# A graph-network kernel on one core: a 25-group ring of source indices, resident destinations, one-hots a group ahead, and the edge products computed during the sums and reloaded in the attention

## The chip, the cores and the metric

The kernel runs on one core of one Trainium2 chip. The metric is device time in microseconds (us); lower is better. The kernel before was timed in three runs: median 12,565.92 us, from 12,555.83 to 12,591.74.

## The reference, cut to what matters

12,500 nodes with 64 features; 400,000 edges, sorted by destination, with 64 attributes each.

```python
def sage_conv(x, src, dst, W_l, b_l, W_r, n_nodes):      # called twice, with a relu between
    msgs = x[src]
    agg = segment_sum(msgs, dst, n_nodes)
    cnt = segment_sum(ones, dst, n_nodes)
    return (agg / maximum(cnt, 1.0)[:, None]) @ W_l.T + b_l + x @ W_r.T

def attention(x, edge_attr, src, dst):                   # 4 heads of 16
    Q, K, V, Ee = x @ Wq.T + bq, x @ Wk.T + bk, x @ Wv.T + bv, edge_attr @ We.T + be
    score = exp(clip((K[src] * Q[dst] * 0.25 * Ee).sum(-1), -5, 5))
    return segment_sum(V[src] * score[..., None], dst, n)

x = layernorm(x + two_sage_convs(x)); out = layernorm(x + attention(x, edge_attr))
```

## The kernel before, in words

A group is 640 edges: 5 for each of the 128 partitions (K = 5). There are 625 groups, in 125 turns of SLOTS = 5, so every buffer that a group uses has five copies, its slots. Nodes are kept on chip in 98 blocks of 128. Since edges are sorted by destination, most groups touch one block of destinations; some touch more. A table made at the start tells each engine a group's first block and how many more it has (97 extra pairs of group and block in all).

The program has three passes over all groups, with dense layers between them.

- **First sum** (`sum_x`) and **second sum** (`sum_h`). SP loads the group's source and destination indices (`edge_ids`). GpSimd (POOL) issues five indirect DMAs, one for each of the five edges of a partition; each gathers 128 rows of a table in DRAM (`x_rows`, then `h_rows`) by the source indices. VectorE (DVE) makes a one-hot matrix `hot` of the destinations inside the block: a subtraction into `dst_local` (L694), then a comparison with `iota` (L695). TensorE (PE) multiplies one-hot and rows, five matmuls (L373). DVE reduces the result (L714), counts degrees in the first sum alone (L716), adds it to the nodes (L717), and goes on to the next pair of group and block. All in one loop (L706) over blocks.
- **Attention** (`att`). POOL gathers K and V rows (`kv_rows`). SP loads indices and edge attributes (`attr`). PE transposes the attributes (L413) and the one-hots (L417), multiplies the attributes by `we2` (L432, L436), fetches the destinations' Q rows by a product with the one-hots (L441, L424), and sums the messages (L446). ScalarE (ACT) copies the transposed pieces and takes the exponent. DVE computes K*Q (L811), times the edge product from PSUM (`kqe`, L812), a reduction (L814), the clip (L815), the one-hot of the group after next (L694, L695), the add to the nodes (L827), and the messages (L820).

Semaphores set the order. `group_done`, counted up by DVE at a group's end, lets SP load the indices of the group that takes the slot; their landing (`ids[u]`) lets POOL gather, and the landing of the five gathers (`got[u]`) lets PE (in the sums) or DVE (in the attention) use them.

## Time and profile before

| what | value |
|---|---|
| median of three timed runs | 12,565.92 us |
| span of the profiled execution | 16,241.9 us |
| its stretches: first sum, second sum, attention | 4,912, 4,898 and 5,978 us |
| what lies before, between and behind them | 459 us |
| POOL busy | 9,186 us (57%) |
| PE busy | 5,274 us (32%) |
| DVE busy | 5,077 us (31%) |

No timed duration of the profiled execution is given beside its span of 16,241.9 us. The span is 29% above the median of the timed runs, so a share of this span is not a share of the timed one. Durations of single instructions, and the distances between them where nothing waits, can be read from it.

### The profile page before, as it was taken

Reading aid. Unit: us, or ns where it says so; the run is one execution under the profiler, and the core shown is the slowest. Engines: PE = TensorE matmul, PEld = TensorE weight load, DVE = VectorE, ACT = ScalarE, POOL = GpSimd, SP = SyncE. Lnnn points to the kernel's source line nnn. Section 1 sums busy time; section 2 is a strip of 40 time slices with the busy share of each in tenths; the row PEclk is TensorE's granted clock in tenths of the full one; section 3 lists DMA queues with packets and bytes.
Section 4 is the critical chain, followed back from the end, with each engine's and each line's share of the span. In section 5 each row is a group of like instructions: output and inputs, shape, how many; then the busy total and the mean of one; then the engine's idle time right before and its main releaser. Section 6 shows DMA issues by size and latency. Waiting matters only on the chain.

```text
span 16241.9 us, 175208 instructions
## 1 busy us (share of the span) xinstructions
PE 5273.6 (32%) x37310; PEld 4336.0 (27%) x37311; DVE 5077.4 (31%) x12457; ACT 1546.3 (10%) x3498; POOL 9186.2 (57%) x9383
## 2 busy tenths in 40 slices
PE   0111111111112111111111113655565566666665
PEld 0000000000002000000000002555555555555555
DVE  3222222222223222222222223333333333333444
ACT  0000000000001000000000000222222222222222
POOL 4666666665564666666656564455555555555554
PEclk9999999999999999999999999766666666666666
DMA  2111111111111111111111111222222122121211
GB/s 50 32 33 32 33 33 32 33 32 31 31 32 36 33 33 32 32 32 32 32 30 32 31 32 27 57 54 54 53 53 54 51 52 52 50 52 49 53 50 50
DMA packets 716290, 649.53 MB, mean 40 GB/s; under 512 B 470247, under 2 KB 566151, under 8 KB 716152
## 3 DMA queue, kind: packets, MB, share of 16 engines
q0 software_dynamic: 300000, 512.60, 13.9%
q1 hardware_dynamic: 416277, 136.79, 3.8%
q8 instruction: 5, 0.08, 0.0%
q14 instruction: 8, 0.07, 0.0%
HBM read 629.36 MB, written 19.26 MB: 40 GB/s over the span
## 4 chain that ended last, share of the span: by engine, by line
issue 31%; DVEq 22%; PE 16%; another core or an unknown queue 15%; DVE 14%; ACT 2%; ACTq 0%; DMA 0%; POOL 0%; SPq 0%; POOLq 0%
DVEq L706 7%; DVE hot L695 5%; PE ps_sum L373 4%; PE ps_sum L446 3%; DVEq L694 3%; DVE part_sum L714 2%; DVE dst_local L694 2%; DVEq L610 2%; DVEq L244 2%; PE ps_e L436 1%; DVEq L712 1%; DVEq L717 1%; PE ps_t L413 1%; DVEq L713 1%
## 5 line engine op out<-in xcount | busy, mean ns | idle before, releaser
L335 POOL DMA_INDIRECT kv<-kv_rows,edge_ids x3125 | 3142.6, 1006 | 3025.2 <-DMA edge_ids<-in_edges 2149.1
L373 PE MATMUL ps_sum<-rows,hot 128*128 128x193 bf16 x7220 | 1396.9, 359 | 8500.1 <-DVE hot L695 5728.5
L335 POOL DMA_INDIRECT rows<-h_rows,edge_ids x3125 | 3025.5, 968 | 1995.7 <-DMA edge_ids<-in_edges 1052.9
L335 POOL DMA_INDIRECT rows<-x_rows,edge_ids x3125 | 3017.1, 965 | 1963.0 <-DMA edge_ids<-in_edges 1001.7
L373 PEld LDWEIGHTS ps_sum<-rows,hot 128*128 128x128 bf16 x7220 | 850.7, 132 | 9045.9 <-issue 9001.2
L694 DVE TENSOR_SCALAR dst_local<-edge_ids,base 128x5 bf16<-128x5 int32 x2265 | 570.4, 252 | 4372.6 <-issue 4337.7
L695 DVE TENSOR_TENSOR hot<-dst_local,iota 128x640 bf16<-128x640 bf16 x2071 | 1713.9, 828 | 377.7 <-issue 249.7
L446 PE MATMUL ps_sum<-message,node_h 128*128 128x64 f32 x6260 | 1203.6, 352 | 272.2 <-issue 235.5
L446 PEld LDWEIGHTS ps_sum<-message,node_h 128*128 128x128 f32 x6260 | 1131.1, 267 | 313.8 <-issue 255.0
L714 DVE TENSOR_REDUCE part_sum<-ps_sum 128x64 f32<-128x192 f32 x1444 | 516.6, 358 | 1924.1 <-issue 1135.8
L550 ACT COPY attrT<-ps_t 128x384 f32<-128x384 f32 x626 | 300.6, 480 | 3295.6 <-remote 1776.6
L436 PE MATMUL ps_e<-we,attrT 128*128 128x128 f32 x2256 | 484.0, 374 | 318.5 <-ACT attrT L550 174.7
L811 DVE TENSOR_TENSOR kq<-kv,ps_q 128x320 f32<-128x320 f32 x375 | 182.9, 488 | 1268.5 <-remote 711.0
L413 PE MATMUL ps_t<-ident,attr 128*128 128x128 f32 x1878 | 480.8, 375 | 273.2 <-issue 266.0
L436 PEld LDWEIGHTS ps_e<-we,attrT 128*128 128x128 f32 x2256 | 457.5, 280 | 354.2 <-ACT attrT L550 193.0
L827 DVE TENSOR_TENSOR node_x<-node_x,ps_sum 128x64 f32 x626 | 137.9, 220 | 1161.1 <-remote 1024.4
L516 ACT ACT_TABLE_LOAD x14 | 18.0, 1283 | 5000.5 <-DVE node_x L725 5000.3
L555 ACT COPY hotT<-ps_hot 128x640 bf16<-128x640 bf16 x626 | 435.4, 696 | 509.5 <-remote 479.8
L516 ACT COPY stage<-node_h 128x896 f32 x14 | 13.2, 943 | 4939.7 <-DVE node_h L725 4939.7
L559 ACT CAST node_h<-hot 128x640 f32<-128x640 bf16 x626 | 447.8, 715 | 0.0
L417 PE MATMUL ps_hot<-ident,hot 128*128 128x128 bf16 x3130 | 407.6, 274 | 90.2 <-issue 83.1
L436 PE MATMUL ps_kv<-we,attrT 128*128 128x128 f32 x1500 | 322.7, 375 | 176.7 <-issue 97.3
(153 smaller groups left out, 6594.4 us busy)
## 6 DMA issues: line engine op xcount, KB each, us to landing
attr<-in_edge_attr SPq DMA_DIRECT2D x627, 160.0 KB
rows<-x_rows,edge_ids POOLq DMA_INDIRECT x3125
rows<-h_rows,edge_ids POOLq DMA_INDIRECT x3125
kv<-kv_rows,edge_ids POOLq DMA_INDIRECT x3125
edge_ids<-in_edges SPq DMA_DIRECT2D x1877, 5.0 KB
kv_rows<-node_h SPq DMA_DIRECT2D x14, 448.0 KB, 3.0
x_rows<-node_q SPq DMA_DIRECT2D x14, 336.0 KB, 2.6
h_rows<-node_q SPq DMA_DIRECT2D x14, 336.0 KB, 2.6
```

What stands on the lines that cost most here:

```text
L335: nc.gpsimd.indirect_dma_start(out=into[:, u, k, 0:width], out_offset=None, in_=table_rows, in_offset=bass.IndirectOffsetOnAxis(ap=edge_id ...
L373: mm = nc.tensor.matmul(ps_sum[:, 0:ROW + 1], hot[:, 0, k, :], rows[:, u, k, 0:ROW + 1], start=(k == 0), stop=(k == K - 1))
L413: tp = nc.tensor.transpose(ps_t[:, i * P:(i + 1) * P], attr[:, u, i * P:(i + 1) * P], ident[:])
L417: tp = nc.tensor.transpose(ps_hot[:, k * P:(k + 1) * P], hot[:, u, k, :], ident16[:])
L436: mm = nc.tensor.matmul(ps_edge[u % 2][:, i * P:(i + 1) * P], attrT[:, i, :], we2[:], start=False, stop=(i == PAIRS - 1))
L446: mm = nc.tensor.matmul(to, one_hots[:, k, :], messages[:, k, :], start=(k == 0), stop=(k == K - 1))
L555: nc.scalar.copy(hotT[:], ps_hot[:, 0:K * P].rearrange("p (i j) -> p i j", i=K)).then_inc(p.hot_c, 1)
L559: nc.scalar.copy(hot32[:, u], hot[:, u])
L694: s.link(v.tensor_scalar(dst_local[:], edge_ids[:, u, K:2 * K], base[:, bass.ds(b, 1)], None, ALU.subtract))
L695: v.tensor_tensor(into, dst_local[:].rearrange("p (k o) -> p k o", o=1).to_broadcast([P, K, P]), iota[:].rearrange("p (o n) -> p o n", o=1 ...
L706: with dve.Fori(0, more + 1) as j:
L714: s.link(v.tensor_reduce(part_sum[:], ps_sum[:, 0:ROW].rearrange("p (s f) -> p f s", s=SPLIT), AX, ALU.add))
```

## The change

**Indices.** The source indices come into a ring of 25 groups (`src_ids`), loaded five groups at a time. The destinations of all groups stay on chip (`dst_ids`, loaded once during the first sum, 25 groups at a time after the first 50). POOL now waits for the slot (`group_done`) itself.

**One-hots.** `one_hot` is one instruction, a scalar_tensor_tensor (subtract, is_equal), in place of two. In the sums it fills the slot of the next group, where before there was one buffer; extra blocks have a path of their own (`hotT`, `ps_extra`).

**Edge products.** Transposes, products and their copies move from the attention into the sums: three groups of edges a turn in the first sum, two a turn in the second. ACT copies the product out of PSUM and stores it to `ee_rows` in DRAM (160 KB a group). The attention loads it back into `ee_in`, in place of the attributes. `kq` takes the space of `attrT`, and `rows` that of `kv`.

```diff
-        edge_ids = sb("edge_ids", [P, SLOTS, 2 * K], I32)
+        src_ids = sb("src_ids", [P, RING, K], I32)
+        dst_ids = sb("dst_ids", [P, (G + AHEAD) * K], I32)
...
             def gather(p, phase, table_rows, into, width):
+                with pool.Fori(0, BIG) as T:
+                    for j in range(SUBS):
+                        pool.wait_ge(ids_in, T * (16 * SUBS) + 16 * (phase * TURNS + j + 1))
+                        for u in range(SLOTS):
+                            at = j * SLOTS + u
+                            pool.wait_ge(p.group_done, T * RING + at + 1)
...
-                        pool.wait_ge(p.ids[u], t * 16 + 16)
...
+                        g = t * SLOTS + u
                         pe.wait_ge(p.got[u], t * (16 * K) + 16 * K)
+                        pe.wait_ge(p.added, g + 1)
+                        pe.wait_ge(p.hot, g + 1)
                         hold(pe)
-                        with pe.Fori(0, more + 1) as j:
...
+                        sum_group(ps_main[u], hot[:, u], u, p.summed)
...
+                        e = first_e + t * per + u
+                        if 0 < u <= per:
+                            edge_products(e - 1)
+                        if u < per:
+                            turn_attr(u, e, (phase * TURNS) * 16 + t * 16 + 16)
...
+            def edge_tiles(first_e, per, turns_before):
+                with act.Fori(0, TURNS) as t:
+                    for i in range(per):
+                        e = first_e + t * per + i
+                        act.wait_ge(ee_turned, e + 1)
+                        act.wait_ge(ee_made, e + 1)
+                        nc.scalar.copy(attrT[:], ps_t[:, 0:PAIRS * P].rearrange("p (i j) -> p i j", i=PAIRS)).then_inc(ee_copied, 1)
+                        act.wait_ge(ee_made, e + 2)
+                        nc.scalar.copy(ee_out[:, i, :], ps_e[:, 0:K * D]).then_inc(ee_ready, 1)
+                        act.wait_ge(ee_ready, e + 2)
+                        nc.scalar.dma_start(ee_v[:, bass.ds(e, 1), :].rearrange("p a c -> p (a c)"), ee_out[:, i, :]).then_inc(ee_stored[i], 16)
...
-            def one_hot(u, b, s, into, ready):
-                s.link(v.tensor_scalar(dst_local[:], edge_ids[:, u, K:2 * K], base[:, bass.ds(b, 1)], None, ALU.subtract))
-                v.tensor_tensor(into, dst_local[:].rearrange("p (k o) -> p k o", o=1).to_broadcast([P, K, P]),
-                                iota[:].rearrange("p (o n) -> p o n", o=1).to_broadcast([P, K, P]), ALU.is_equal).then_inc(ready, 1)
+            def one_hot(g, b, into, ready):
+                v.scalar_tensor_tensor(into, dst_ids[:, bass.ds(g * K, K)].rearrange("p (k o) -> p k o", o=1).to_broadcast([P, K, P]),
+                                       base[:, bass.ds(b, 1)], iota[:].rearrange("p (o n) -> p o n", o=1).to_broadcast([P, K, P]),
+                                       ALU.subtract, ALU.is_equal).then_inc(ready, 1)
...
+            def sum_turn(p, t, nodes, count_edges):
+                words = group_words(ENG.DVE, t, 0, SLOTS + 1)
+                for u in range(SLOTS):
+                    before, first, more = words[u]
+                    g = t * SLOTS + u
+                    one_hot(g + 1, block_at(words[u + 1][1]), hot[:, (u + 1) % SLOTS], p.hot)
+                    dve.wait_ge(p.added, g + 2)
+                    dve.wait_ge(p.summed, g + 1)
+                    add_rows(block_at(first), ps_main[u], nodes, count_edges, p.step, g + 1, p.added)
...
-                v.tensor_tensor(kqe[:], kq[:], ps_edge[u % 2][:, 0:K * D].rearrange("p (k f) -> p k f", k=K), ALU.mult).then_inc(p.scored, 1)
+                v.tensor_tensor(kqe[:], kq, ee_in[:, u], ALU.mult).then_inc(p.scored, 1)
```

How instructions stand on the engines at the places that matter. DVE in the first sum, from one group's add to the next one-hot; ISA and REGISTER_ALU are the sequencer's own steps. Before:

```order
L717 TENSOR_TENSOR node_x<-node_x,part_sum 128x64
L706 REGISTER_ALU x3
L706 COMPARE_AND_BRANCH
L719 ISA
L706 UNCONDITIONAL_BRANCH [waits sx_ids1]
L706 ISA
L694 REGISTER_ALU
L694 ISA
L694 TENSOR_SCALAR dst_local<-edge_ids,base 128x5
L610 ISA
L695 TENSOR_TENSOR hot<-dst_local,iota 128x640 [waits sx_step]
```

After, at the same place (the extra blocks' path between L836 and L847 is jumped over when there are none):

```order
L839 COMPARE_AND_BRANCH
L836 UNCONDITIONAL_BRANCH
L847 ISA
L812 ISA
L812 REGISTER_ALU
L812 ISA
L812 SCALAR_TENSOR_TENSOR hot<-dst_ids,base,iota 128x640
L833 REGISTER_ALU
L818 TENSOR_REDUCE part_sum<-ps_q 128x64 [waits sx_summed,sx_added]
```

The loop head, the wait for indices and the small subtraction have gone from between the add and the one-hot.

PE in the first sum, from the landing of the gathered rows on. Before:

```order
L367 UNCONDITIONAL_BRANCH [waits sx_got1]
L367 ISA
L373 MATMUL ps_sum<-rows,hot 128x193 [waits sx_hot,sx_added]
L373 MATMUL ps_sum<-rows,hot 128x193 x4
L367 REGISTER_ALU x3
```

After (`edge_space` holds the attributes):

```order
L475 REGISTER_ALU [waits sx_got1]
L444 MATMUL ps_q<-kv,hot 128x193 [waits sx_added,sx_hot]
L444 MATMUL ps_q<-kv,hot 128x193 x4
...
L459 MATMUL ps_e<-be_parts,ones 128x384 [waits ee_ready]
L460 REGISTER_ALU
L462 MATMUL ps_e<-we,attrT 128x128 [waits ee_copied]
L462 MATMUL ps_e<-we,attrT 128x128 x2
L453 MATMUL ps_t<-ident,edge_space 128x128 [waits ee_copied,attr_in1]
L453 MATMUL ps_t<-ident,edge_space 128x128 x2
```

One loop head less stands ahead of the group's matmuls, and the edge work stands behind them.

DVE in the attention, after the change:

```order
L1010 REGISTER_ALU [waits att_ee0]
L953 TENSOR_TENSOR attrT<-kv,ps_q 128x320 [waits att_query]
L726 ISA
L954 TENSOR_TENSOR kqe<-attrT,edge_space 128x320 [waits att_step]
L955 REGISTER_ALU
L956 TENSOR_REDUCE score<-kqe 128x20 [waits att_scored]
L726 REGISTER_ALU
L957 TENSOR_SCALAR clipped<-score 128x20 [waits att_step]
```

The same order as before up to the clip, but `kqe` now reads both its inputs from on-chip memory (`attrT` holds `kq`, `edge_space` holds `ee_in`), where the second was PSUM; behind the clip stands the single one-hot instruction.

## Rows read from the trace of the kernel before

**Rows 1.** Groups of instructions by line, POOL's three.

```profile
L335 POOL DMA_INDIRECT kv<-kv_rows,edge_ids x3125 | 3142.6, 1006 | 3025.2 <-DMA edge_ids<-in_edges 2149.1 <-issue 876.1
L335 POOL DMA_INDIRECT rows<-h_rows,edge_ids x3125 | 3025.5, 968 | 1995.7 <-DMA edge_ids<-in_edges 1052.9 <-issue 942.8
L335 POOL DMA_INDIRECT rows<-x_rows,edge_ids x3125 | 3017.1, 965 | 1963.0 <-DMA edge_ids<-in_edges 1001.7 <-issue 961.3
```

**Rows 2.** The chain of waits, one of DVE's sequencer steps in the first sum.

```profile
3006.08 0.70 DVEq L713
```

**Rows 3.** Timeline, POOL alone, first and last of twelve gathers in a row.

```profile
105.39 0.95 POOL L335 DMA_INDIRECT rows<-x_rows,edge_ids  x1 [0.30 <-issue]
...
119.16 0.95 POOL L335 DMA_INDIRECT rows<-x_rows,edge_ids  x1 [0.30 <-issue]
```

**Rows 4.** Windows before, between and behind the three passes.

```profile
0.00:88.00 88.00, 0.87 (x6) 0.67 (x7) 52.65 (x84) 0.02 (x1) 1.07 (x8) 1.00 0.44 112
4981.00:5091.00 110.00, 71.51 (x319) 63.77 (x319) 69.15 (x124) 43.81 (x42) 0.94 (x1) 1.00 0.16 45
10003.00:10217.00 214.00, 159.49 (x608) 140.87 (x608) 113.87 (x231) 60.71 (x114) 0.15 (x1) 1.00 0.11 31
16195.00:16242.00 47.00, 0.00 (x0) 0.00 (x0) 29.70 (x50) 7.92 (x13) 0.00 (x0) 0.50 0.31 68
```

**Rows 5.** Timeline of the second sum, one group's round on three engines.

```profile
5106.25 1.11 POOL L335 DMA_INDIRECT rows<-h_rows,edge_ids  x1 [0.31 <-issue]
...
5109.45 0.97 PE L373 MATMUL ps_sum<-rows,hot 128*128 128x193 bf16 x5 [5.45 <-DMA rows<-h_rows,edge_ids]
...
5110.52 0.36 DVE L714 TENSOR_REDUCE part_sum<-ps_sum 128x64 f32<-128x192 f32 x1 [3.98 <-issue]
5111.03 0.23 DVE L717 TENSOR_TENSOR node_h<-node_h,part_sum 128x64 f32 x1
...
5112.13 0.83 DVE L695 TENSOR_TENSOR hot<-dst_local,iota 128x640 bf16<-128x640 bf16 x1
...
5112.67 1.11 POOL L335 DMA_INDIRECT rows<-h_rows,edge_ids  x1 [0.30 <-issue]
```

**Rows 6.** Timeline of the first sum, one group's round on PE and DVE.

```profile
102.78 0.97 PE L373 MATMUL ps_sum<-rows,hot 128*128 128x193 bf16 x5 [68.62 <-issue]
...
105.57 0.82 DVE L695 TENSOR_TENSOR hot<-dst_local,iota 128x640 bf16<-128x640 bf16 x1
```

**Rows 7.** Timeline of the attention: first group's last gather and use, a blocked gather.

```profile
10223.41 0.95 POOL L335 DMA_INDIRECT kv<-kv_rows,edge_ids  x1 [0.31 <-issue]
...
10226.21 0.49 DVE L811 TENSOR_TENSOR kq<-kv,ps_q 128x320 f32<-128x320 f32 x1 [5.17 <-DMA kv<-kv_rows,edge_ids]
...
10504.72 0.48 DVE L820 TENSOR_TENSOR message<-kv,weight 128x320 f32<-128x320 f32 x1
10504.92 1.11 POOL L335 DMA_INDIRECT kv<-kv_rows,edge_ids  x1 [0.30 <-issue]
```

**Rows 8.** Timeline of the attention, one group's round on DVE without waits.

```profile
10256.94 0.48 DVE L811 TENSOR_TENSOR kq<-kv,ps_q 128x320 f32<-128x320 f32 x1
10257.46 0.49 DVE L812 TENSOR_TENSOR kqe<-kq,ps_e 128x320 f32<-128x320 f32 x1
...
10258.50 0.18 DVE L815 TENSOR_SCALAR clipped<-score 128x20 f32<-128x20 f32 x1
10258.86 0.23 DVE L694 TENSOR_SCALAR dst_local<-edge_ids,base 128x5 bf16<-128x5 int32 x1 [0.18 <-issue]
10259.12 0.82 DVE L695 TENSOR_TENSOR hot<-dst_local,iota 128x640 bf16<-128x640 bf16 x1
...
10260.03 0.49 DVE L820 TENSOR_TENSOR message<-kv,weight 128x320 f32<-128x320 f32 x1
```

**Rows 9.** Timeline, end of the program: a scalar_tensor_tensor.

```profile
16210.31 0.63 DVE L735 SCALAR_TENSOR_TENSOR node_x<-total,node_x 128x448 f32 x1
```

**Rows 10.** Windows, the attention as a whole.

```profile
10217.00:16195.00 5978.00, 3653.52 (x29202) 3285.20 (x29202) 2315.07 (x5500) 1433.87 (x3328) 3142.61 (x3125) 0.65 0.20 52
```

More of the change, by code:

```diff
@@ L193, in __init__ @@
                 self.step = sem(f"{name}_step")
-                if name == "att":
-                    self.attr_t = sem("att_attr_t")
-                    self.attr_c = sem("att_attr_c")
-                    self.edge = sem("att_edge")
+                if name != "att":
+                    self.x_hot, self.x_summed, self.x_added, self.x_step = (
+                        sem(f"{name}_x_{n}") for n in ("hot", "summed", "added", "step"))
+                else:
+                    self.ee = [sem(f"att_ee{u}") for u in range(SLOTS)]
                     self.hot_t = sem("att_hot_t")
@@ L285, in load_edges, with feed_attention, products @@
+            def feed_attention(p):
+                for i, count in enumerate((2 * TURNS, 2 * TURNS, TURNS)):
+                    sp.wait_ge(ee_stored[i], 16 * count)
+                loads = SUBS + 2 * TURNS
+                def products(t):
                     for u in range(SLOTS):
                         sp.wait_ge(p.group_done, t * SLOTS + u + 1)
-                        sp.dma_start(edge_ids[:, u, :], edges_v[:, bass.ds(t * SLOTS + u, 1), :].rearrange("p a c -> p (a c)")).then_inc(p.ids[u], 16)
@@ L298, in _ @@
-            store_rows(d_split, x_rows_v, node_q)
-            load_edges(sum_x)
+                        sp.dma_start(ee_in[:, u].rearrange("p k f -> p (k f)"),
+                                     ee_v[:, bass.ds(t * SLOTS + u, 1), :].rearrange("p a c -> p (a c)")).then_inc(p.ee[u], 16)
+                products(0)
+                with sp.Fori(0, BIG - 1) as T:
+                    for j in range(SUBS):
+                        t = T * SUBS + j + 1
+                        products(t)
+                        load_sources(j, t - 1 + SUBS, t - 1 + loads)
@@ L300, in _ @@
+                with sp.Fori(TURNS - SUBS + 1, TURNS) as t:
+                    products(t)
             sp.wait_ge(be_stored, 16)
@@ L633, in _ @@
             v.engine_nop().then_inc(att.scored, 1)
+            for s in (ee_copied, ee_made, ee_ready, sum_x.added, sum_h.added, sum_x.x_added, sum_h.x_added):
+                v.engine_nop().then_inc(s, 1)
             v.engine_nop().then_inc(extra.added, 1)
```

298 lines of the change are left out of this document (177 added, 121 removed).

## The prediction

> **What bounds the kernel now.** I read the groups of instructions first, then the windows between the passes, then the timeline.
>
> POOL is the busiest engine, with 9,375 indirect DMAs, five a group in each pass. The reader is to see both columns of [rows 1]: means of 965, 968 and 1,006 ns, and idle time before them that is mostly put down to the landing of `edge_ids`, 1,001.7 + 1,052.9 + 2,149.1 = 4,204 us. Read by itself this says: take the wait for the indices away. But the span is 16,242 us and the timed median 12,566 us, so at least 3,676 us of this execution are not in the timed runs. The chain of waits shows where such time sits: in some stretches each step of DVE's sequencer takes 0.70 us, as [rows 2], and the groups behind them end late. `group_done` and the index loads are late with them, so POOL's waits for indices are this execution's symptom.
>
> So I build the timed run from POOL running freely. Twelve gathers in a row start from 105.39 to 119.16 us, 1.252 us apart (about 0.947 busy, 0.305 between) [rows 3]. 9,375 x 1.252 = 11,737 us. Outside the passes POOL stands still for 88 + 110 + 214 + 47 = 459 us [rows 4]. Sum 12,196 us. The median is 12,566, so 370 us are left for all waits and slow gathers together: 370 / 1,875 = 0.20 us a group and pass. POOL is at work in 93% of the timed run. The profiled execution checks this: its gathers took 9,185.2 us against 9,375 x 0.947 = 8,878, an excess of 307 us [rows 1], though POOL waited so often. Made against its own span of 16,242 us, the same sum is 9,185 busy, 2,780 of issue and short idle, 4,204 put down to indices (some of it the stretches between the passes), and the rest at both ends. The change must be priced against the timed 12,566.
>
> **Where the excess comes from.** A gather that starts while DVE is inside a one-hot is stretched. At 5112.67 POOL starts, 0.54 us after the comparison of 5112.13, which runs to 5112.96. That gather takes 1.11 in place of 0.95 us; a gather that starts before the comparison isn't touched, and one at 5106.25 shows the same 1.11 a group earlier [rows 5]. So POOL's gather needs something at about 0.13 us from its start, and gets it when DVE ends: excess = what is left of the DVE instruction, less 0.13 us. In the attention the message product does it too: it starts at 10504.72, POOL 0.20 later, and 0.48 - 0.20 - 0.13 = 0.15 predicts the 1.11 us seen [rows 7]. The comparison and the messages both read two operands from on-chip memory.
>
> The Trainium skill, "SBUF — State Buffer", section "Who interferes with whom", states just this: a DVE instruction with two SBUF inputs contends with a GpSimd instruction that reads SBUF, and whoever is second blocks fully. The trace agrees (1.11 us against 0.95). By that page the new `kqe`, whose second input moves from PSUM to SBUF, becomes one more blocker, which speaks against this change; the sum below gets the same from the message rows.
>
> **The change part by part, on POOL's clock.**
>
> *Gathers*: 9,375 before and after, same rows, same bytes, 11,737 us. Nothing of the change touches this term.
>
> *Waits for indices*: gone, worth next to nothing. A group's chain without waits takes about 3.6 us in the attention (L811 to the end of L820, 10256.94 to 10260.52) [rows 8] against 6.26 us of POOL. With five slots the indices land long before POOL wants them. What hides this load is the lead of about four groups, 25 us; without it, a load's latency would show at each group. At the three starts of passes I take 1 us each; the bounds are 0 and 3 us.
>
> *Start-up*: SP now sends the six `be_parts` loads, a destination load of 6,400 small pieces and five source loads ahead of the row stores. The stores are paced by DVE inside the first 88 us [rows 4], so this is mostly covered. No row has such a load; bounds 0 and +40 us, I take +2, since DVE's 52.65 busy us there cover it.
>
> *Small subtraction (L694)*: off DVE, 0.23 us a time. DVE waits for PE here anyway; the gain in time is 0. Its effect is on when the one-hot starts.
>
> *One-hot as one instruction*: the nearest row is L735, 448 elements in 0.63 us; at DVE's rate of one element per 1.04 ns (the comparison's 640 in 0.83) the new one lasts 0.83 us as well [rows 5, 9]. It still reads two operands on chip, so it still blocks.
>
> *When it starts*: this is the term that decides the sums. In the second sum I count from the end of a group's last gather, 5106.25 + 1.11 = 5107.36: PE starts 2.09 later, DVE's reduction at 3.16, the add at 3.67, the comparison at 4.77 [rows 5]. POOL's next starts are 0.305 + n x 1.252, so 4.06 and 5.31. The latter is 0.54 inside the comparison: excess 0.83 - 0.54 - 0.13 = 0.16 a group. In the first sum the distance from PE to the comparison is 2.79 in place of 2.68 [rows 5, 6], so the excess is 0.27. In the attention, L811 starts 1.85 after the end of the group's last gather (10223.41 + 0.95 to 10226.21) [rows 7], and POOL's starts fall at 0.96, 2.21 and 3.46 after L811; the one-hot is at 2.18 [rows 8], so this is on the edge. What is left of the 370 us, 370 - 625 x (0.27 + 0.16) = 101 us, is 0.16 a group there.
>
> After: a loop head and a subtraction less between the add and the one-hot. Of the 1.10 us between them [rows 5] I take off 0.27 for the subtraction and 0.25 for the loop head: 0.57. On PE a loop head less saves about 0.28. One-hot at 4.77 - 0.28 - 0.53 = 3.96 in the second sum, 4.07 in the first, against POOL's start at 4.06. That is the other edge: a hair before it and the excess is 0.6 us, a hair behind and it is 0. Landings scatter by more than 0.1 us, so I take half of each: 0.30 and 0.25. If the added edge work brings PE to its faster level, its burst of 0.97 us shrinks, the one-hot starts at about 3.5 and 3.65, and the excess is 0.15 to 0.29. Either way about 0.5 for both sums together, against 0.43 before. Bounds: 0 and 1.2.
>
> *Attention*: the one-hot starts 0.30 behind the clip's start, 1.86 after L811, and POOL's start at 2.21 is 0.35 inside it: excess 0.35. `kqe` (0.49 us, at 0.52) meets POOL's 0.96 at its very end: 0; at a random phase it costs (0.49 - 0.18)^2 / (2 x 1.252) = 0.04, at worst 0.31. I take 0.30 for the pass, against 0.16. Bounds 0 and 0.7.
>
> *Edge work moved into the sums* (transposes, products, two ACT copies, a store): at most 5 us a group of PE in a round of 6.26 in which PE ran 0.97 us [rows 5]. Nothing waits for it. In the attention it frees PE, which was busy 3,654 of 5,978 us at a mean granted clock of 0.65 [rows 10], 5.8 us a group: close to POOL's 6.26, but below it, so little comes of that. The reload of 160 KB takes the place of the attributes' load.
>
> Sum: 12,566 + 625 x ((0.55 + 0.30) - (0.43 + 0.16)) = 12,566 + 162; with phases at random (each one-hot costing (0.83 - 0.18)^2 / 2.504 = 0.17 before and after) only the 0.04 of `kqe` is left, +25. Between the two, with -1 for starts: about **12,650 us**.
>
> **The rivals.**
>
> *One-hots fall between the gathers* (faster). If the new one-hot starts 0.1 us later than I count, each POOL start in the sums is clear of it: -0.43 x 625 = -269 us, and with +60 for the attention about 12,360. For it: 3.96 and 4.07 are within 0.1 us of the edge, and one more sequencer step does it. Against: it needs both sums.
>
> *The indices' wait was real in part, or PE was* (faster). Then up to the whole 370 us go, less what stays of the blocking; about 12,330. For it: 4,204 us of waits in [rows 1], PE's 5.8 us a group in [rows 10]. Against: the free-running sum plus the blocking already fills 12,566.
>
> *Nothing changes* (same): random phases, 12,590.
>
> *The sums lock onto the bad side* (much slower): the one-hot starts just before a gather in nearly all groups; 1.2 in place of 0.43: +480, about 13,040. It decides from a start before 4.0 us.
>
> A measurement of this kernel can tell about 0.3% (38 us) from no change.
>
> **How the numbers follow.** Somewhat more blocking 0.45 (its own range 12,600 to 12,800, so 0.05 of it is "same"); between the gathers 0.18; real waits 0.12; nothing 0.20, of which a part lies either side; bad side 0.05. Faster 0.31, same 0.23, slower 0.46. The range reaches from the faster rivals to beyond the likeliest: 12,330 to 12,850 us.
>
> **What the changed profile would show.** POOL's 9,375 gathers, no wait for indices, and if my bound is right hardly a gain from that. Means of the gathers: about 990 to 1,010 ns in the sums (0.947 plus 0.05 to 0.06), where 965 was read before, and over 1,006 in the attention. Gathers stretched under `kqe` (L954), which never was so before. PE no longer transposes attributes in the attention. What would make the prediction wrong: a free gather that isn't 1.252 us apart in the timed runs, or one-hots that start elsewhere than 3.9 to 4.1 us after a group's last gather.

## The result, and the profile after

The changed kernel takes 12,867.71 us (median of 4 runs, 12,850.10 to 12,876.80); the kernel before took 12,567.24 (4 runs, three of them the ones given ahead of the prediction). The ratio is 1.0231, 95% interval 1.0217 to 1.0246: slower by 300 us. The forecast was 12,650, slower; the direction is right, the size is 218 us too small, and the time lies 18 us above the range.

The profiled execution of the changed kernel spans 12,848.3 us, so this time the profile is of an execution like the timed ones. The groups of instructions that answer to [rows 1], with the new one-hot below them (columns: busy us, mean ns of one, idle us before them and what ended it), and then the page's chain of what ended last, by engine:

```profile
L417 POOL DMA_INDIRECT kv<-kv_rows,src_ids x3125 | 3242.9, 1038 | 1155.4 <-issue 1141.1 <-DMA src_ids<-in_edges 8.2 <-DVEq L1022 6.1
L417 POOL DMA_INDIRECT kv<-h_rows,src_ids x3125 | 3174.6, 1016 | 1047.9 <-issue 1008.6 <-DVEq L847 39.3
L417 POOL DMA_INDIRECT kv<-x_rows,src_ids x3125 | 3123.3, 999 | 1038.3 <-issue 997.8 <-DVEq L847 40.5
...
L812 DVE SCALAR_TENSOR_TENSOR hot<-dst_ids,base,iota 128x640 bf16<-128x640 bf16 (+1 forms) x1879 | 1668.5, 888 | 1094.8 <-issue 983.9 <-DVE node_x L822 46.4 <-DVE node_h L822 44.6
```

```profile
POOL 62%; issue 23%; DMA 5%; PE 4%; DVE 3%; DVEq 1%; POOLq 1%; ACT 0%; SPq 0%; ACTq 0%
```

The reader is to see that nearly all of the 4,204 us of waits for indices of [rows 1] are gone (8.2 us are left, in steps no longer than the usual 0.3 us between two gathers), and that 85% of the chain is GpSimd (POOL) and the time in which it gets its next instruction ready. In the passes no gather starts more than 0.32 us after the end of the one before it. So the span is a sum of POOL's own times. A gather that nothing stretches takes 0.944 us, with 0.305 to the next: 9,375 x 1.249 = 11,709 us. Outside the passes POOL stands for 88 + 96 + 203 + 64 = 451 us. The rest is in the means: 999, 1,016 and 1,038 ns, not 944. That is 3,123.3 - 2,950, 3,174.6 - 2,950 and 3,242.9 - 2,950, together 691 us, or 0.277, 0.359 and 0.469 us a group in first sum, second sum and attention. 11,709 + 451 + 691 = 12,851 us, against a span of 12,848.

Where a gather is stretched is seen in the second sum, in the timeline (start us, us, engine, line):

```profile
6005.77 0.94 POOL L417 DMA_INDIRECT kv<-h_rows,src_ids  x1 [0.30 <-DVEq L847]
6006.05 0.88 DVE L812 SCALAR_TENSOR_TENSOR hot<-dst_ids,base,iota 128x640 bf16<-128x640 bf16 x1 [0.42 <-issue]
...
6009.69 0.97 PE L444 MATMUL ps_q<-kv,hot 128*128 128x193 bf16 x5 [3.30 <-DMA kv<-h_rows,src_ids]
...
6010.76 0.36 DVE L818 TENSOR_REDUCE part_sum<-ps_q 128x64 f32<-128x192 f32 x1 [3.83 <-PE ps_q L444]
6011.27 0.23 DVE L822 TENSOR_TENSOR node_h<-node_h,part_sum 128x64 f32 x1
6011.90 0.89 DVE L812 SCALAR_TENSOR_TENSOR hot<-dst_ids,base,iota 128x640 bf16<-128x640 bf16 x1 [0.41 <-issue]
6012.01 1.60 POOL L417 DMA_INDIRECT kv<-h_rows,src_ids  x1 [0.30 <-issue]
6013.91 0.94 POOL L417 DMA_INDIRECT kv<-h_rows,src_ids  x1 [0.30 <-issue]
```

At 6005.77 the gather starts 0.28 us ahead of the one-hot and takes 0.94. At 6012.01 it starts 0.11 us behind the one-hot's start and takes 1.60: it ends 0.82 us after the one-hot's end (6012.79). These are the two sides of an edge. Over the 6,795 one-hots, main and extra, that have a next gather in this trace and in those of its two repetitions below, by the distance from the one-hot's start to the start of the next gather (the first one that starts no more than 0.4 us ahead of it):

| gather starts after the one-hot by | median duration of that gather |
|---|---|
| -0.2 to 0.1 us | 0.944 us |
| 0.1 to 0.2 | 1.562 |
| 0.3 to 0.4 | 1.345 |
| 0.5 to 0.6 | 1.162 |
| 0.7 to 0.8 | 0.980 |
| 0.8 to 0.9 | 0.944 |

In every blocked row the median gather ends 0.818 us behind the one-hot's end. Of the five gathers of a group the fourth has three quarters of the excess or more: 207, 315 and 371 ns a group in the three passes. It starts 4.05 us after the last gather of the group before; the one-hot starts 3.96 us after it in the first sum, 3.93 in the second and 3.75 to 3.81 in the slots of the attention (medians).

Put down to the instruction that ends 0.818 us (within 0.02) ahead of the gather's end, the excess of the changed kernel divides so. Of the 1,837 gathers that took over 12 ns more than 0.944 us, 13 have no such instruction.

| us a group | first sum | second sum | attention |
|---|---|---|---|
| one-hot of a group's first block | 0.209 | 0.299 | 0.376 |
| one-hots of its extra blocks | 0.061 | 0.058 | 0.030 |
| message | | | 0.043 |
| `kqe` | | | 0.022 |

### The profile page after: what moved, and what is told of

The parts are those of the page before. It is cut to its first block, busy times and chain, and to the rows that moved or that the text cites. A ratio compares the mean times of both kernels' runs of the same rounds, so it can differ in the third digit from the quotient of the medians.

```text
span 12848.3 us, 163168 instructions
## 1 busy us (share of the span) xinstructions
PE 5759.9 (45%) x37300; PEld 5027.3 (39%) x37301; DVE 4596.1 (36%) x10194; ACT 2041.0 (16%) x4233; POOL 9541.9 (74%) x9383
## 4 chain that ended last, share of the span: by engine, by line
POOL 62%; issue 23%; DMA 5%; PE 4%; DVE 3%; DVEq 1%; POOLq 1%; ACT 0%; SPq 0%; ACTq 0%
POOL kv L417 62%; DMA kv<-x_rows,src_ids 2%; DMA kv<-h_rows,src_ids 1%; DMA kv<-kv_rows,src_ids 1%; PE ps_t L548 1%; PE ps_q L503 1%; PE ps_q L444 0%; PE ps_sum L444 0%; PE ps_sum L548 0%; DMA src_ids<-in_edges 0%; POOLq L414 0%; DVE node_h L812 0%; PE ps_t L497 0%; PE ps_kv L518 0%; DVE kqe L954 0%
## 5 line engine op out<-in xcount | busy, mean ns | idle before, releaser
L417 POOL DMA_INDIRECT kv<-kv_rows,src_ids x3125 | 3242.9, 1038 | 1155.4 <-issue 1141.1
L417 POOL DMA_INDIRECT kv<-h_rows,src_ids x3125 | 3174.6, 1016 | 1047.9 <-issue 1008.6
L417 POOL DMA_INDIRECT kv<-x_rows,src_ids x3125 | 3123.3, 999 | 1038.3 <-issue 997.8
L812 DVE SCALAR_TENSOR_TENSOR hot<-dst_ids,base,iota 128x640 bf16<-128x640 bf16 (+1 forms) x1879 | 1668.5, 888 | 1094.8 <-issue 983.9
L444 PE MATMUL ps_q<-kv,hot 128*128 128x193 bf16 x2500 | 477.4, 355 | 2019.4 <-DMA kv<-h_rows,src_ids 1052.9
L444 PE MATMUL ps_sum<-kv,hot 128*128 128x193 bf16 x2500 | 466.2, 349 | 2031.9 <-DMA kv<-x_rows,src_ids 994.9
L462 PEld LDWEIGHTS ps_e<-we,attrT 128*128 128x128 f32 x3750 | 910.2, 325 | 10.9 <-ACT attrT L645 2.1
L462 PE MATMUL ps_e<-we,attrT 128*128 128x128 f32 x3750 | 901.5, 411 | 1.2 <-ACT attrT L645 1.1
L818 DVE TENSOR_REDUCE part_sum<-ps_sum 128x64 f32<-128x192 f32 x500 | 178.6, 357 | 1514.3 <-PE ps_sum L444 1514.1
L527 PEld LDWEIGHTS ps_hot<-ident,hot 128*128 128x128 bf16 x3130 | 303.7, 137 | 786.2 <-issue 784.8
```

Source lines behind the costliest of these rows:

```text
L417: nc.gpsimd.indirect_dma_start(out=into[:, u, k, 0:width], out_offset=None, in_=table_rows, in_offset=bass.IndirectOffsetOnAxis(ap=src_ids ...
L444: mm = nc.tensor.matmul(to[:, 0:ROW + 1], one_hots[:, k, :], rows[:, u, k, 0:ROW + 1], start=(k == 0), stop=(k == K - 1))
L462: mm = nc.tensor.matmul(ps_e[:, pair * P:(pair + 1) * P], attrT[:, pair, :], we2[:], start=False, stop=(pair == PAIRS - 1))
L527: tp = nc.tensor.transpose(ps_hot[:, k * P:(k + 1) * P], hot[:, u, k, :], ident16[:])
L812: v.scalar_tensor_tensor(into, dst_ids[:, bass.ds(g * K, K)].rearrange("p (k o) -> p k o", o=1).to_broadcast([P, K, P]), base[:, bass.ds(b ...
L818: v.tensor_reduce(part_sum[:], sums[:, 0:ROW].rearrange("p (s f) -> p f s", s=SPLIT), AX, ALU.add).then_inc(step, 1)
```

## The experiments

Theory A is that of the forecast: a gather stands still while a VectorE (DVE) instruction with two SBUF inputs runs, if it starts inside it, and the place of the one-hot in POOL's round makes the time. Rival B: DVE's longer or greater work, wherever it stands. Rival B2: the edge work and its transfers in the sums.

**The changed kernel again (after_again, after_third).** These and all kernels below, whether made from the changed kernel or from the one before, carry one bitwise instruction more where a group's word is unpacked.

> The changed kernel with one more bitwise instruction in the unpacking of a group's word, nothing else: the one to compare the others with. Both theories: 12,868 us within 20.

> The changed kernel again, as in after_again, to stand beside the others of this set, since the place of the one-hot against the gathers was 0.1 us apart between the two sets before (3.93 and 4.03 us in the second sum) and the time 75 us. Between 12,790 and 12,870 us.

12,792.38 us (12,779.36 to 12,804.64) and 12,787.85 us (12,781.68 to 12,793.16), where before took 12,648.76 and 12,645.24: ratios 1.0113 (1.0096 to 1.0130) and 1.0111 (1.0094 to 1.0127). So after_again missed its 20 us, and the change costs 1.1% there, 2.3% in the first set. The traces say how: the one-hot of the second sum starts at 4.03 us in its round, not at 3.93, and that pass has 0.224 and 0.222 us a group of excess in place of 0.359; the attention has 0.560 and 0.544 in place of 0.469. PE starts 0.06 us later too (1.77 against 1.71). Between the two profiled executions the spans differ by 46 us and the excess by 44, so the blocking is nearly all of the difference. Whether the extra instruction or another chip moved the one-hot was not separated; the kernel before, without the extra instruction, took 80 us more in these sets than in the first. That 0.1 us of one-hot comes with 75 us of time speaks for A; it doesn't show it.

**No edge work in the sums (no_edge_work).**

```diff
                 def attrs(t):
+                    return
...
-                        if 0 < u <= per:
-                            edge_products(e - 1)
-                        if u < per:
-                            turn_attr(u, e, (phase * TURNS) * 16 + t * 16 + 16)
...
-            edge_tiles(0, EE_A, 0)
-            edge_tiles(EE_A * TURNS, EE_B, TURNS)
```

> The changed kernel without the edge work of the sums: no loads of attributes there, no transposes, products, copies or stores of them; the attention loads the attributes themselves in the place of the products, so the product with We is left out of the result. Theory A: within 40 us of the changed kernel, since the one-hots keep their place (PE's waits may move them a little). Rival B2 (the edge work and its DMA traffic are what the sums lose by): 100 to 400 us less, at most 12,760.

12,792.98 us against 12,792.38: rival B2 falls. The windows of the two sums and the attention, first of no_edge_work, then of the changed kernel as it was first profiled (stretch, its length, then busy us of PE, PE's weight loads, DVE, ACT, POOL; granted clock of PE, DMA share, GB/s):

```profile
100.00:4200.00 4100.00, 741.66 (x3801) 465.14 (x3802) 1148.50 (x2954) 30.36 (x29) 3089.39 (x3119) 1.00 0.20 39
4300.00:8400.00 4100.00, 781.77 (x3944) 503.32 (x3944) 1122.62 (x2266) 35.39 (x51) 3038.61 (x3078) 1.00 0.19 38
8600.00:12700.00 4100.00, 2733.04 (x22191) 2556.87 (x22191) 2109.01 (x4515) 1181.20 (x2608) 3179.97 (x3020) 1.00 0.28 73
```

```profile
100.00:4200.00 4100.00, 1514.95 (x7469) 1239.50 (x7470) 1132.49 (x2931) 507.39 (x885) 3113.27 (x3119) 0.56 0.27 68
4300.00:8400.00 4100.00, 1237.72 (x6093) 964.08 (x6093) 1064.28 (x2167) 226.63 (x499) 3142.55 (x3097) 0.53 0.23 57
8600.00:12800.00 4200.00, 2799.85 (x22888) 2639.19 (x22888) 2151.54 (x4669) 1218.27 (x2693) 3234.79 (x3117) 0.50 0.27 73
```

PE and ACT do 773 and 477 us more in the first sum, DMA 29 GB/s more, and the time is the same. The excess is the same too: 0.239, 0.220 and 0.546 us a group without the edge work, 0.236, 0.222 and 0.544 in after_third.

The clock of 1.00 in the first three rows is not a reading. The trace of no_edge_work holds no record of the granted clock at all, and the view prints 1.00 where it has none. The matmuls of the messages tell more (line, busy us, mean ns; no_edge_work, the changed kernel, the kernel before):

```profile
L539 PE MATMUL ps_sum<-message,node_h 128*128 128x64 f32 x6260 | 1478.4, 423 | 0.2 <-DVE message L951 0.2
```

```profile
L548 PE MATMUL ps_sum<-message,node_h 128*128 128x64 f32 x6260 | 1469.3, 422 | 0.3 <-DVE message L962 0.3
```

```profile
L446 PE MATMUL ps_sum<-message,node_h 128*128 128x64 f32 x6260 | 1203.6, 352 | 272.2 <-issue 235.5 <-DVE message L820 33.9
```

They take as long without the edge work as with it at a granted 0.50 (the lower level, 1.2 GHz), and less in the kernel before, whose clock in the attention was granted at 0.65 on average [rows 10].

**A memset ahead of the one-hot (hot_later, hot_later_2).** 256 and 448 elements, in the sums only.

```diff
+                    v.memset(mid[:, 0:4, :], 0.0)
                     one_hot(g + 1, block_at(words[u + 1][1]), hot[:, (u + 1) % SLOTS], p.hot)
```

> The changed kernel with a VectorE memset of some 0.25 us ahead of each one-hot of the two sums; the attention is as it was. Theory A (a gather that starts while a VectorE instruction with two SBUF inputs runs stands until that one ends, and in the sums it is the place of the one-hot, 0.1 us ahead of the fourth gather of a group, that makes the time): the one-hot now starts 0.1 us or more behind the start of that gather, so most of the 0.28 and 0.36 us a group are gone, 625 x 0.55 = 340 us less, about 12,530. Rival B (the gathers take longer because VectorE does more and longer work in all, wherever it stands; or edge products and their transfers slow them): no change or some us more, 12,870 to 12,890.

> The changed kernel with a memset of 448 elements (some 0.47 us) ahead of each one-hot of the sums. The memset of 256 moved the one-hot by 0.03 us only, since 0.26 of its 0.27 us lay in the time in which VectorE's sequencer gets the one-hot ready anyway; this one should move it by some 0.22 us, to about 4.2 us after the group's last gather, behind the start of the fourth at 4.06. Theory A: most of the sums' excess goes, 0.15 us or more of each sum's 0.22 to 0.36, so 190 us or more below after_third. Rival B (amount of VectorE work, not its place): not below it, if anything above.

12,755.93 us (36 below after_again) and 12,754.77 us (33 below after_third): neither reached what A expected. The trace of hot_later_2 shows that the edit did not do what it was for:

```profile
6005.65 0.23 DVE L822 TENSOR_TENSOR node_h<-node_h,part_sum 128x64 f32 x1
6006.11 0.43 DVE L831 MEMSET mid<- 128x448 f32 x1 [0.23 <-issue]
6006.46 0.76 DVE L812 SCALAR_TENSOR_TENSOR hot<-dst_ids,base,iota 128x640 bf16<-128x640 bf16 x1
6006.48 1.56 POOL L417 DMA_INDIRECT kv<-h_rows,src_ids  x1 [0.30 <-issue]
```

The memset lies in the 0.4 us and more in which DVE's sequencer gets the one-hot ready. The one-hot's record starts later (in the second slot of the second sum at 4.15 us in its round against 3.97 in after_third, medians) but is shorter, 0.76 us against 0.885, so its end stayed where it was: 4.91 against 4.90.

It is the end that counts: in after, after_third, hot_later_2 and two_step_hot alike every gather that starts 0.15 to 0.79 us ahead of the end of a one-hot is stretched (4,685 of them), and of the 1,460 that start 0.85 to 0.90 us ahead of it two are, whether the one-hot's record has 0.76, 0.83 or 0.885 us. So the excess fell little, 0.236 and 0.222 to 0.206 and 0.204 us a group, 30 us in all. Against B: 540 us more of DVE work (1,250 memsets of 432 ns) made the kernel 33 us faster, not slower. Since the one-hots didn't move, neither run tests A. A gather that starts 0.1 to 0.25 us into this memset, 0.1 us or more ahead of the one-hot's start, takes 0.944 us.

**The one-hot of before (two_step_hot).**

```diff
-                v.scalar_tensor_tensor(into, dst_ids[:, bass.ds(g * K, K)].rearrange("p (k o) -> p k o", o=1).to_broadcast([P, K, P]),
...
+                v.tensor_scalar(dst_local[:, slot], dst_ids[:, bass.ds(g * K, K)], base[:, bass.ds(b, 1)], None, ALU.subtract).then_inc(made, 1)
+                dve.wait_ge(made, count)
+                v.tensor_tensor(into, dst_local[:, slot].rearrange("p (k o) -> p k o", o=1).to_broadcast([P, K, P]),
+                                iota[:].rearrange("p (o n) -> p o n", o=1).to_broadcast([P, K, P]), ALU.is_equal).then_inc(ready, 1)
```

> The changed kernel with the one-hot of before: a subtraction of 5 elements, a wait for it, then the comparison of 640 elements, 0.83 us in place of 0.885. Theory A: the comparison starts 0.2 to 0.3 us later in a round than the single instruction, so in the sums it falls behind the fourth gather's start and in the attention nearer to it: 150 to 300 us below after_third. Rival B: more VectorE time in all (some 0.2 us a group), so not below; rival C (the single instruction blocks by its length alone): 0.05 us x 1,875 x the blocked share, at most 50 us below.

12,574.18 us (12,571.81 to 12,578.46): 214 us below after_third, and 0.9940 of before (0.9924 to 0.9957). POOL's groups and DVE's two steps:

```profile
L420 POOL DMA_INDIRECT kv<-kv_rows,src_ids x3125 | 3151.5, 1008 | 1155.3 <-issue 1144.9 <-DVEq L1026 5.8 <-DMA src_ids<-in_edges 4.6
L420 POOL DMA_INDIRECT kv<-h_rows,src_ids x3125 | 3062.4, 980 | 1048.1 <-issue 963.0 <-DVEq L851 85.1
L420 POOL DMA_INDIRECT kv<-x_rows,src_ids x3125 | 3055.4, 978 | 1038.3 <-issue 976.1 <-DVEq L851 62.2
...
L817 DVE TENSOR_TENSOR hot<-dst_local,iota 128x640 bf16<-128x640 bf16 x1879 | 1553.3, 827 | 65.0
L815 DVE TENSOR_SCALAR dst_local<-dst_ids,base 128x5 bf16 (+1 forms) x2267 | 553.4, 244 | 1179.7 <-issue 984.8 <-DVE node_h L826 78.0 <-DVE node_x L826 77.4
```

DVE works more (553 us of subtractions, against a comparison shorter by 0.058 us), and yet 207 us of POOL's excess are gone: 0.17, 0.18 and 0.32 us a group. B and C (the length) fall. The second and fourth slot of the second sum in three traces:

| kernel | one-hot starts in its round, slots 2 and 4 | excess of the group after it |
|---|---|---|
| changed | 3.91, 3.91 us | 0.415, 0.471 us |
| after_third | 3.97, 3.98 | 0.220, 0.202 |
| two_step_hot | 4.28, 4.29 | 0.035, 0.039 |

These two slots are the ones that gain. In the first, third and fifth the group after the one-hot has 0.50, 0.19 and 0.11 us in two_step_hot and 0.37, 0.17 and 0.13 in after_third; what is left in either sum is nearly all under main one-hots, and over half of it in the first of these slots.

In the attention the comparison starts at 4.15 to 4.23 in place of 3.81 to 3.98, mostly behind the fourth gather's start, and the message behind it becomes the next to block (388 gathers and 0.088 us a group, against 143 and 0.035 in after_third):

```profile
10506.92 0.23 DVE L815 TENSOR_SCALAR dst_local<-dst_ids,base 128x5 bf16 x1
...
10507.14 0.94 POOL L420 DMA_INDIRECT kv<-kv_rows,src_ids  x1 [0.30 <-issue]
10507.18 0.82 DVE L817 TENSOR_TENSOR hot<-dst_local,iota 128x640 bf16<-128x640 bf16 x1
...
10508.33 0.48 DVE L966 TENSOR_TENSOR message<-kv,weight 128x320 f32<-128x320 f32 x1
10508.39 1.25 POOL L420 DMA_INDIRECT kv<-kv_rows,src_ids  x1 [0.31 <-issue]
```

**The second input taken out of SBUF (iota_in_psum, before_iota_in_psum).**

```diff
+        iota_s = ps_t[:, 512:512 + P]
+        iota_a = ps_kv[:, 0:P]
...
-            def one_hot(g, b, into, ready):
+            def one_hot(g, b, into, ready, numbers=iota_s):
...
+            st.link(v.tensor_copy(iota_s, iota[:]))
             sum_pairs(sum_h, node_h, False, False)
```

> The changed kernel whose one-hots read the column numbers from a copy in PSUM, so that they have one SBUF input instead of two; they stay as long or get longer. Theory A: the one-hots block no gather any more: 0.28 and 0.36 us a group of the sums and 0.235 of the attention's 0.47, in all 625 x 0.80 = 500 us less (what add_rows and kqe still block stays), about 12,370. Rival B: no change, 12,870.

> The kernel of before whose one-hots read the column numbers from PSUM (extra sums of the attention stand in another bank for it). Theory A: its gathers go free too but for kqe and the message: 12,187 of the same edit on the changed kernel and some 30 us for the longer gaps between the passes, 12,200 to 12,230. Rival: if the other parts of the change (edge products in the sums, ids ahead) are worth or cost something of their own, this one ends over 100 us away from 12,187.

12,187.29 us (12,185.80 to 12,189.49), 605 us below after_again and 0.9637 of before (0.9621 to 0.9654). The same edit on the kernel of before (which also moves the sums of its extra blocks to another bank of PSUM and gives PE one wait more for it): 12,207.72 us, 0.9652 (0.9636 to 0.9668), 438 us below its before and inside what was expected. Groups of POOL and of the two forms of one-hot in iota_in_psum, and then POOL's in before_iota_in_psum:

```profile
L419 POOL DMA_INDIRECT kv<-kv_rows,src_ids x3125 | 2978.1, 953 | 1154.9 <-issue 1074.1 <-DVEq L1027 75.6 <-DMA src_ids<-in_edges 5.2
L419 POOL DMA_INDIRECT kv<-h_rows,src_ids x3125 | 2952.8, 945 | 1047.6 <-issue 950.7 <-DVEq L849 96.9
L419 POOL DMA_INDIRECT kv<-x_rows,src_ids x3125 | 2951.0, 944 | 1037.6 <-issue 971.8 <-DVEq L849 65.8
...
L814 DVE SCALAR_TENSOR_TENSOR hot<-dst_ids,base,ps_t 128x640 bf16<-128x640 f32 (+1 forms) x1252 | 1102.2, 880 | 1057.0 <-issue 966.9 <-DVE node_h L824 44.6 <-DVE node_x L824 44.1
L814 DVE SCALAR_TENSOR_TENSOR hot<-dst_ids,base,ps_kv 128x640 bf16<-128x640 f32 (+1 forms) x627 | 552.0, 881 | 51.0 <-issue 27.0 <-DVE ps_kv L953 0.9
```

```profile
L336 POOL DMA_INDIRECT kv<-kv_rows,edge_ids x3125 | 2978.9, 953 | 1159.9 <-issue 947.5 <-DMA edge_ids<-in_edges 212.4
L336 POOL DMA_INDIRECT rows<-x_rows,edge_ids x3125 | 2953.0, 945 | 1038.1 <-issue 940.0 <-DMA edge_ids<-in_edges 98.1
L336 POOL DMA_INDIRECT rows<-h_rows,edge_ids x3125 | 2951.8, 945 | 1049.5 <-issue 950.2 <-DMA edge_ids<-in_edges 99.3
```

The one-hot is as long as ever (880 ns), and next to nothing of the sums' excess is left (0.002 and 0.005 us a group). The one-hots still meet the gathers: 1,293 gathers start 0.1 to 0.7 us inside one, with a median of 0.945 us and none above 0.961. In after_again 1,273 start there, and all of them are stretched, with a median of 1.44. A is shown. The saving is 605 us and not the 500 expected: the main and extra one-hots of after_again cost 590 us, since those of the attention took 0.475 us a group where 0.235 had been expected, more than the sums fell short by; the rest is mostly `kqe` and the message, which meet the gathers less (0.045 us a group are left in the attention).

With hardly anything blocked the two kernels are 20 us apart, and their ratios to the kernel before, taken in two sets, overlap (0.9621 to 0.9654 and 0.9636 to 0.9668). So ring, resident destinations, early one-hots and moved edge work together are worth about nothing here. And some 438 of before's 12,645 us were its own blocking.

**Three sets that took a quarter longer.** In these every kernel, the one of before included, took 15,242 to 16,365 us, so they are read by their ratios alone, and only for what they are. What slowed them is not known.

The kernel of before (but for the one bitwise instruction) was run in each of them for its trace:

> The kernel of before with the one more bitwise instruction of after_again. It shows where the gathers of before are blocked when nothing else slows the execution. 12,645 us within 20 on the chip of the two sets before, 12,567 on the first. Theory A: its comparison of 640 elements starts 4.15 us or later after the last gather of a group in the sums, so that about 0.2 us a group of each sum is lost, as in two_step_hot, and the rest (0.3 us a group or more) in the attention.

> before_again once more: in that set every kernel, the one of before too, took 16,000 us in place of 12,600, with GpSimd waiting 900 to 1,900 us a pass, so it couldn't show an undisturbed round of before. Theory A, where the kernel of before takes some 12,600: no waits of GpSimd; an excess of 0.15 to 0.3 us a group in each sum and 0.15 to 0.35 in the attention, in all 0.7 us a group (about 440 us); the comparison starts later in its round than the 3.93 to 4.03 us of the changed kernel's single instruction.

> before_again a third time, since the two sets before took 16,000 us with every kernel. Theory A, where the kernel of before takes some 12,600: no waits of GpSimd; an excess of 0.15 to 0.3 us a group in each sum and 0.15 to 0.35 in the attention, in all 0.7 us a group (about 440 us); the comparison starts later in its round than the 3.93 to 4.03 us of the changed kernel's single instruction.

The kernel of before with the single instruction, all else as it was:

```diff
-                s.link(v.tensor_scalar(dst_local[:], edge_ids[:, u, K:2 * K], base[:, bass.ds(b, 1)], None, ALU.subtract))
-                v.tensor_tensor(into, dst_local[:].rearrange("p (k o) -> p k o", o=1).to_broadcast([P, K, P]),
+                v.scalar_tensor_tensor(into, edge_ids[:, u, K:2 * K].rearrange("p (k o) -> p k o", o=1).to_broadcast([P, K, P]),
```

> The kernel of before with only the one-hot of the changed kernel: one scalar_tensor_tensor of 0.885 us in place of a subtraction, a wait and a comparison; ids, edge products and all else as before. Theory A: the instruction that blocks starts some 0.2 us earlier in a round and so falls on the start of the fourth gather more often: 60 to 200 us above before_again. Rival (the slower time of the changed kernel comes from its ring of ids, the one-hots a group ahead, or the edge work): within 30 us of before_again, or below it.

> before_single_hot once more (before, with only the one-hot made by one scalar_tensor_tensor). Theory A, where the kernel of before takes some 12,600: 60 to 200 us above before_again_2, since the blocking instruction comes 0.2 us earlier in a round. Rival: within 30 us of it, or below.

> before_single_hot a third time. Theory A, where the kernel of before takes some 12,600: 60 to 200 us above before_again_3. In the two disturbed sets it was 1.4% and 1.3% below its neighbour, where the blocking in the attention had fallen from 0.28 to 0.18 us a group; if that holds here as well, the single instruction alone does not cost before what it costs the changed kernel, and the theory keeps only the changed kernel's own place of it.

iota_in_psum with three more operands in PSUM:

```diff
+        kq = ps_kv[:, P:P + K * D].rearrange("p (k f) -> p k f", k=K)
+        weight = ps_t[:, 0:K * HEADS]
+        part_sum = ps_t[:, 512 + P:512 + P + D]
```

> iota_in_psum, and in PSUM also the product of keys and queries, the weights and the sums of the three parts, so that no VectorE instruction of a round has two SBUF inputs. Theory A: what kqe and the message still block (28 us of the third pass) goes: 12,160, if PSUM operands don't make the instructions longer than their cover; rival: 12,187 or more, since other things end the gathers.

> all_in_psum once more. Theory A: 12,160 (12,187 less the 28 us that kqe and the message still blocked). Rival: 12,187 or more.

> all_in_psum a third time. Theory A: 12,160 (12,187 less the 28 us that kqe and the message still blocked). Rival: 12,187 or more.

And two_step_hot once more:

> two_step_hot again, on whichever chip this is, beside the kernel of before and its single-instruction form: with single_hot_2 and before_again_2 it says what the form of the one-hot costs in either kernel. Theory A: about 70 us below before_again_2, as in the set before (12,574 against 12,645).

| ratio to before (95% interval) | first set | second set | third set |
|---|---|---|---|
| before_again | 1.0085 (1.0065 to 1.0106) | 1.0093 (1.0065 to 1.0121) | 1.0098 (1.0068 to 1.0128) |
| single one-hot in before | 0.9939 (0.9915 to 0.9964) | 0.9966 (0.9951 to 0.9981) | 0.9963 (0.9950 to 0.9977) |
| all_in_psum | 0.9538 (0.9519 to 0.9557) | 0.9506 (0.9482 to 0.9530) | 0.9479 (0.9455 to 0.9503) |
| two_step_hot_2 | | 0.9489 (0.9461 to 0.9516) | |

POOL's groups of before_again_3, of single_hot_3 and of all_in_psum_3:

```profile
L335 POOL DMA_INDIRECT kv<-kv_rows,edge_ids x3125 | 3154.4, 1009 | 2996.7 <-DMA edge_ids<-in_edges 2119.3 <-issue 877.4
L335 POOL DMA_INDIRECT rows<-h_rows,edge_ids x3125 | 3032.8, 971 | 2019.3 <-DMA edge_ids<-in_edges 1057.8 <-issue 961.5
```

```profile
L335 POOL DMA_INDIRECT rows<-h_rows,edge_ids x3125 | 3068.7, 982 | 1860.3 <-issue 971.9 <-DMA edge_ids<-in_edges 888.4
L335 POOL DMA_INDIRECT kv<-kv_rows,edge_ids x3125 | 3062.7, 980 | 3087.4 <-DMA edge_ids<-in_edges 2216.7 <-issue 870.7
```

```profile
L419 POOL DMA_INDIRECT kv<-h_rows,src_ids x3125 | 2950.8, 944 | 1819.5 <-issue 1053.2 <-DVEq L849 766.4
L419 POOL DMA_INDIRECT kv<-kv_rows,src_ids x3125 | 2947.7, 943 | 2683.7 <-DVEq L1027 1628.4 <-issue 1038.2 <-DMA src_ids<-in_edges 17.1
```

Here POOL waits: 680 to 2,220 us a pass for indices or for `group_done`, as in [rows 1]. What can be read: with no VectorE instruction of a round left that reads two SBUF inputs, the gathers take 943 or 944 ns in every pass, so none is stretched, in the attention neither; the 12,160 us expected of it in an ordinary set were not measured.

Where POOL waits, both forms of the changed kernel that were run are ahead: two_step_hot_2, with its blocking, gets 0.949, and taking all blocking away (0.951 in the same set) gives nothing more. (two_step_hot_2 was expected about 70 us below before_again_2; it is 997.) Which part of the change brings that, and what the changed kernel as it stands would take there, was not run.

The single one-hot in before was expected to be slower, for executions of 12,600 us; it is 1.3 to 1.4% below before_again in all three sets. (before_again itself is 0.9 to 1.0% above the kernel of before, so there the bitwise instruction has a price of its own.) In the second sum its blocking grew (982 against 971 ns) and in the attention it fell (980 against 1,009), while POOL's wait for indices shrank in the second sum (888 against 1,058 us) and grew in the attention (2,217 against 2,119). What it does to before in an ordinary execution stays open, as does where in its rounds before is blocked there.

## Why the forecast was right in kind and short in size

**What bounds the kernel.** Right. POOL running freely, 1.252 us a gather, was measured as 1.249 in an undisturbed execution. The 459 us outside the passes were measured as 451, partly by luck: 47 us had been taken for the tail, but POOL's last gather of the kernel before ended 71 us ahead of the end, so before had 483 us there, and 346 us and not 370 for waits and slow gathers. The reading that the waits for indices of [rows 1] are worth nothing in the timed runs is borne out: they are gone, and the kernel got slower; before_iota_in_psum, which still loads its ids as before, has next to none either (its 98.1, 99.3 and 212.4 us hold the stretches of 88, 98 and 203 us ahead of and between the passes).

**The mechanism.** Right, and shown. "What is left of the DVE instruction, less 0.13 us" gives 0.885 - 0.11 - 0.13 = 0.65 for the gather at 6012.01, which took 0.66 more than 0.944. The means of the gathers were to be 990 to 1,010 ns in the sums and over 1,006 in the attention, and were 999, 1,016 and 1,038.

**The sums.** The one-hot's start was placed at 3.96 (second) and 4.07 us (first) and is at 3.93 and 3.96; the gather's at 4.06 is at 4.05. "Half of each: 0.30 and 0.25" gave 0.55 us; measured are 0.359 + 0.277 = 0.636, 54 us more. The main one-hots have 0.299 and 0.209 of it, no more than was taken for them, and that is in part luck: in the second sum the excess isn't half everywhere, but 0.33 to 0.50 us in the groups behind four slots and 0.06 behind the fifth, and the length was taken as 0.83 where it is 0.885 us. What is above the forecast are the one-hots of the extra blocks, 0.119 us or 74 us in both sums, for which the prediction's sum has no term.

**The attention** is the term most mis-sized: 0.30 us a group taken (my own number was 0.35), 0.469 measured, 106 us more. The main one-hot has 0.376 of it (the gather starts 0.24 to 0.30 us inside it, not 0.35, and it is 0.055 us longer); the message with 0.043, the extra one-hots with 0.030 and `kqe` with 0.022 stand beside it, of which only `kqe` had been weighed for the changed kernel, at 0 to 0.04. That `kqe` becomes a blocker, as the Trainium skill has it ("SBUF — State Buffer", "Who interferes with whom"), is true here: 171 gathers, 13.7 us. The other half of that section of the Trainium skill, that an instruction with one SBUF input (outside VectorE's 2-port modes) doesn't contend, agrees with iota_in_psum (944 and 945 ns).

**The steps that failed** are two. One is the size of the blocking, 0.55 + 0.30 us a group where 1.105 were measured: mostly the attention's 0.30, which was 0.469, and the extra blocks' one-hots in the sums, taken at nothing. The other is "between the two": the sum by its own terms was 12,566 + 162 = 12,728, and it was drawn down to 12,650 half-way to random phases. The phases aren't random: each one-hot follows the landing of its round by the same chain, and in four of five slots of the second sum its median start lies between 3.91 and 3.95 us. The account of the 218 us: 78 for the drawing down, 159 for the three terms of excess, 17 for the median above the profiled execution, less 36 since the free-running sum came to 12,160 and not 12,196 (gaps of 96 and 203 us where [rows 4] had 110 and 214, a tail of 64 where 47 had been taken, and 0.003 us a gather).

**Costed at nothing, and nothing:** the edge work (12,793 with and without it), the start-up (first gather at 88.1 us), the indices. **Wrong on the side:** that the edge work might bring PE to its faster level. With it the granted clock is 0.56, 0.53 and 0.50 in the three stretches, near the lower level, and the five matmuls of a group have about the same mean with it, without it and in the kernel before (349 to 359 ns). In the attention the matmuls of the messages even got slower than before, 422 against 352 ns, and it cost nothing, since PE is not what POOL waits for.

**The rivals.** "Between the gathers" needed the one-hot 0.1 us later. Moved by some 0.3 us, by two_step_hot, it does end faster than before, by 0.6%; but 0.35 us a group stay in the sums and 0.32 in the attention. Its price had a slip: the attention's 0.30 against 0.16 is 88 us and not 60. "Real waits" may hold in the three long sets, where two forms of the changed kernel are 5% ahead, and not in the timed ones. "Bad side" was right in direction and 172 us too dear.

## What to carry to other kernels

Where GpSimd's indirect DMAs are the bound, look first at what the longest VectorE instruction with two SBUF inputs does to them, and move one input to PSUM: here that took 4.7% off this kernel and 3.5% off the one before it, more than everything else that the change did. Until that is done, an edit that moves such an instruction is timed with the blocking that it brings or takes away (0.1 us came with 0.6% here, 0.3 us with 1.7%), so an edit's own worth can't be read from the time. And when a sum by terms has been worked out from a fixed round, don't average it with random phases.

## What was not expected of the hardware

The blocked gather ends 0.818 us behind the end of the VectorE instruction, to the nanosecond in the medians of seven classes of distance, whatever was left of it. The window in which a start is caught is 0.10 to 0.75 us into an instruction of 0.885 us. Just ahead of that window it is the one-hot that gives way: where a gather starts 0.03 to 0.10 us behind it, the gather takes 0.944 us as ever and the one-hot up to 0.95 in place of 0.885, the longer the later the gather starts. In hot_later_2 a memset of 0.43 us in front of the one-hot moved its end by 0.01 us. Taking one input of a 640-element scalar_tensor_tensor from PSUM in fp32 in place of SBUF in bf16 doesn't change its length (880 against 885 ns).
